# Where the second norm's transposes, its scale and two chunks of dequantisation stand in the order of an attention and feed-forward kernel

## What is computed

```python
x = x + attention(layernorm(x))     # first norm, "n1"
x = x + ffn(layernorm(x))           # second norm, "n2"

# attention, per batch and chunk of 128 tokens, 4 heads of 128
q, k, v = x @ Wq + bq, x @ Wk + bk, x @ Wv + bv
k = k / max(norm(k), 1e-12)
beta, alpha = softplus(x @ Wbeta + bbeta), sigmoid(x @ Walpha + balpha)
cla = cumsum(log(alpha + 1e-6))                  # within the chunk
attn = (q @ k.T) * beta.T * where(causal, exp(cla - cla.T), 0)
y_local = attn @ v
y = y_local + (q @ state.T) * exp(cla)
state = state * exp(cla_end) + v.T @ (k * beta * exp(cla_end - cla))

# feed-forward, 4-bit weights with a scale for 32 numbers, 4096 hidden
gate, up = x @ Wg.T, x @ Wu.T
out = (gelu_tanh(gate) * up) @ Wd.T
```

## Time and profile before

| | us |
|---|---|
| median of 3 runs | 1176.11 (1175.02 to 1176.43) |
| the profiled execution | 1177.4 |
| its span, first to last instruction | 1175.6 |
| TensorE busy with matmuls | 1152.5 (98%) |
| VectorE busy | 838.0 (71%) |
| GpSimd (POOL) busy | 503.1 (43%) |
| ScalarE busy | 394.8 (34%) |

### The profile page before, as it was taken

One profiled execution on the slowest core, in us unless ns is written; L12 is line 12 of the kernel. 1 busy time (PEld: TensorE's weight loads), 2 busy tenths in 40 slices (PEclk: granted clock), 3 DMA queues, 4 the chain that ended last, 5 costly groups with the idle time before them and its releaser, 6 DMA issues.

```text
span 1175.6 us, 19512 instructions
## 1 busy us (share of the span) xinstructions
PE 1152.5 (98%) x7756; PEld 757.4 (64%) x7756; DVE 838.0 (71%) x1387; ACT 394.8 (34%) x831; POOL 503.1 (43%) x503
## 2 busy tenths in 40 slices
PE   6999999999989999999999999999999999999998
PEld 3565554656534444777777777777777777777775
DVE  7778554544865664887788778877887787777554
ACT  3343432433332232333333333333333333332221
POOL 3267232322445773425542563366335634462110
PEclk9999999999999999999999999999999999999999
DMA  8012000000010001110011001100110011000111
GB/s 295 2 47 82 22 24 28 19 14 5 20 54 18 19 18 37 33 41 19 19 37 37 19 19 37 37 19 19 37 37 19 19 37 37 19 23 23 37 37 63
DMA packets 22635, 41.94 MB, mean 36 GB/s; under 512 B 2640, under 2 KB 2704, under 8 KB 22544
## 3 DMA queue, kind: packets, MB, share of 16 engines
q1 hardware_dynamic: 22544, 40.70, 10.7%
HBM read 36.46 MB, written 4.23 MB: 35 GB/s over the span
## 4 chain that ended last, share of the span: by engine, by line
PE 90%; DVE 5%; POOL 2%; issue 1%; ACT 1%; DMA 1%; SPq 0%; DVEq 0%; POOLq 0%
PE ps L445 37%; PE ps L472 27%; PE ps L408 14%; PE ps L313 7%; PE ps L282 1%; DVE bigA L774 1%; PE ps L367 1%; POOL WR L1188 1%; DMA WR<-wqkv 1%; PE ps L361 1%; POOL kn_s L1156 1%; PE ps L350 1%; PE ps L374 0%; DVE wf L963 0%; DVE X L887 0%
## 5 line engine op out<-in xcount | busy, mean ns | idle before, releaser
L472 PE MATMUL ps<-WR,ihl_s 128*128 128x512 f16 x816 | 185.9, 379 | 0.0
L408 PE MATMUL ps<-XT,WR 128*128 128x512 f16 x768 | 172.0, 382 | 3.0 <-DVE X L928 3.0
L472 PE MATMUL ps<-WR,vv 128*128 128x512 f16 x720 | 164.7, 379 | 0.0
L445 PE MATMUL ps<-XT,WR 128*128 128x256 f16 x1152 | 157.1, 273 | 0.0
L445 PE MATMUL ps<-REG,WR 128*128 128x256 f16 x1152 | 157.1, 273 | 0.0
L928 DVE SCALAR_TENSOR_TENSOR X<-ps,X 128x512 f32<-128x512 f32 x128 | 88.0, 689 | 79.0 <-PE ps L472 76.9
L408 PEld LDWEIGHTS ps<-XT,WR 128*128 128x128 f16 x768 | 75.4, 98 | 94.7 <-DVE X L928 3.5
L472 PEld LDWEIGHTS ps<-WR,ihl_s 128*128 128x128 f16 x816 | 79.9, 98 | 85.3
L445 PEld LDWEIGHTS ps<-XT,WR 128*128 128x128 f16 x1152 | 112.7, 98 | 33.5
L1172 POOL TENSOR_TENSOR ihl_s<-fw,ihl_s 128x512 f16<-128x512 f32 x51 | 63.5, 1264 | 136.1 <-ACT ihl_s L606 136.1
L445 PEld LDWEIGHTS ps<-REG,WR 128*128 128x128 f16 x1152 | 112.7, 98 | 13.0
(11 more groups left out here) (166 smaller groups left out, 1874.1 us busy)
## 6 DMA issues: line engine op xcount, KB each, us to landing
load<-codes SPq DMA_DIRECT2D x48, 256.0 KB
load<-scales SPq DMA_DIRECT2D x48, 256.0 KB
y<-X SPq DMA_DIRECT2D x16, 256.0 KB, 2.0
bigA<-cla SPq DMA_DIRECT2D x14, 256.0 KB, 3.2
WR<-wqkv SPq DMA_DIRECT2D x3, 1024.0 KB, 10.9
X<-x SPq DMA_DIRECT2D x3, 1024.0 KB, 13.1
X<-x SPq DMA_DIRECT2D x4, 256.0 KB, 3.4
bigC<-bv SPq DMA_DIRECT2D x1, 256.0 KB, 5.8
```

The source lines that it names most:

```text
L408: mm = eng.matmul(bank[:, :], buf[:, wp, o + kt, 128 * j:128 * j + 128], XT[:, xp, kt, 512 * b:512 * b + 512], start=(n == 0), stop=(n == 11))
L445: mm = eng.matmul(half_bank(kind, name), w(wp, kt), x(xp, kt), start=(n == 0), stop=(n == 5))
L472: mm = eng.matmul(PS[bank][:, :], ih[:, ip, 128 * tt:128 * tt + 128], buf[:, wp, 8 + j, :], start=(m == 0), stop=(m == 11))
```

## The change

TensorE: in the steps T = 5 to 7 and 9 to 11 the transposes follow all projections and the tile; at T = 8 and 12 they follow the projections and three of the four down products, at T = 4 they stay behind the first two projections. Behind the loop they stand between the second and the third down product. ScalarE and VectorE take their halves in the matching order. POOL makes the norm's scale as the first thing in `head`. The dequantisation of chunks 6 and 7 moves from behind the loop into the steps T = 13 and 14, with the bit instructions of chunks 6, 7 and 8 at the ends of the steps T = 12, 13 and 14.

```diff
+DEQUANTED = (0, 1, 2, 3, 5, 7, 13, 14)
@@ TensorE
                 head(T)
                 if T == 0:
                     decay(1)
-                for f in fill[:2]:
-                    qkv(*f)
-                if not fill:
+                if i >= 0 and i % 4 == 0:
+                    for f in fill[:2]:
+                        qkv(*f)
+                    if i == 0:
+                        turn("n2", T - 1)
+                    for f in fill[2:]:
+                        qkv(*f)
+                    if i > 0:
+                        for tt in range(3):
+                            down(i // 4 - 1, tt)
+                        turn("n2", T - 1)
+                        down(i // 4 - 1, 3)
                     upgate(i)
-                if T >= 1:
-                    turn("n2", T - 1)
-                for f in fill[2:]:
-                    qkv(*f)
-                if i > 0 and i % 4 == 0:
-                    for tt in range(4):
-                        down(i // 4 - 1, tt)
-                if i >= 0 and fill:
-                    upgate(i)
+                else:
+                    for f in fill:
+                        qkv(*f)
+                    if i > 0:
+                        upgate(i)
+                    if T >= 1:
+                        turn("n2", T - 1)
                 mid(T)
-            for tt in range(3):
+            for tt in range(2):
                 down(2, tt)
             turn("n2", NT - 1)
-            down(2, 3)
+            for tt in range(2, 4):
+                down(2, tt)
@@ ScalarE
-                if T >= 1:
-                    turn("n2", T - 1)
                 for f in fill:
                     project(*f)
+                if T >= 4 and T % 4 == 0:
+                    turn("n2", T - 1)
                 if T >= 4:
                     act_tile(T - 4)
-                if T in (0, 1, 2, 3, 5, 7):
+                if T % 4:
+                    turn("n2", T - 1)
+                if T in DEQUANTED:
                     dequant(dk)
                     dk += 1
-            dequant(6)
             turn("n2", NT - 1)
-            dequant(7)
@@ VectorE
                 weigh(T)
-                for f in fill[:2]:
-                    project(*f)
-                if T >= 1:
-                    turn_low("n2", T - 1)
-                for f in fill[2:]:
-                    project(*f)
-                if i > 0 and i % 4 == 0:
-                    for tt in range(4):
-                        gather(i // 4 - 1, tt)
-                if i >= 0:
+                if i >= 0 and i % 4 == 0:
+                    for f in fill[:2]:
+                        project(*f)
+                    if i == 0:
+                        turn_low("n2", T - 1)
+                    for f in fill[2:]:
+                        project(*f)
+                    if i > 0:
+                        for tt in range(3):
+                            gather(i // 4 - 1, tt)
+                        turn_low("n2", T - 1)
+                        gather(i // 4 - 1, 3)
                     act_tile(i)
-                if T in (0, 1, 2, 3, 5, 7):
+                else:
+                    for f in fill:
+                        project(*f)
+                    if i > 0:
+                        act_tile(i)
+                    if T >= 1:
+                        turn_low("n2", T - 1)
+                if T in DEQUANTED:
                     dq_finish(dk)
                     dk += 1
                 mid(T)
-                if T in (0, 1, 2, 4, 6):
+                if T in (0, 1, 2, 4, 6, 12, 13, 14):
                     dq_bits(dk)
-            dq_bits(6)
-            dq_finish(6)
             apply("n2", NT - 1)
-            dq_bits(7)
+            for tt in range(2):
+                gather(2, tt)
             turn_low("n2", NT - 1)
-            for tt in range(3):
+            for tt in range(2, 4):
                 gather(2, tt)
-            dq_finish(7)
-            gather(2, 3)
             for i in range(12, 32):
-                if i == 12:
-                    dq_bits(8)
                 act_tile(i)
@@ GpSimd, in head(T)
+                if T >= 1:
+                    norm_scale("n2", T - 1)
                 pl.wait_ge(s_ss, T + 1)
...
-                if T >= 1:
-                    norm_scale("n2", T - 1)
                 pl.wait_ge(s_mask, T + 1)
@@ SyncE
-                if T in (0, 1, 2, 3, 5, 7):
+                if T in DEQUANTED:
                     load_chunk(k)
                     k += 1
-            for k in range(8, 48):
+            for k in range(10, 48):
                 load_chunk(k)
```

## The result

| | before, us | after, us |
|---|---|---|
| median of 7 runs each | 1176.24 | 1179.34 |
| the profiled execution, its span | 1177.4, 1175.6 | 1178.5, 1176.8 |

The changed kernel is slower: the ratio is 1.0027, with a 95% interval from 1.0015 to 1.0039. That is 3.1 us more, where 3.8 less were forecast, and it lies outside the range.

A forecast was written before the change was run, and what follows sets the result against it. TensorE, busy 98% of the span, was taken as the bound, so only its waits could be gained. 5.2 - 0.15 - 1.3 = 3.75 us gained gave 1172.4 us, range 1168.5 to 1175.8.

The forecast's parts named there:

- Part 1: Loop, T = 5 to 12: transposes moved later no longer wait for VectorE's normalised rows; 5.2 us gained.
- the second PSUM use and the low half: VectorE's low half ends some 2.9 us after the tile, its PSUM bank is retaken at 4.5: hidden, 1.6 us spare.
- Part 2: POOL's scale ahead of k's scaling: 5.1 us from statistics to attention weighting's end; first four steps gain 0.15 us.
- the stretch: Lengthening of POOL's six small instructions beside VectorE's four bit instructions: 0.7 us taken, bounds 0 and 1.0.
- Part 3: Dequantisation in T = 12 to 14: removes tile 12's 2.99 us wait, brings some 6 us new; loses 1.3 us.
- rival (b): POOL's stretch above 1.0, about 1.2, or a late last transpose: 1.2 us gained, 1174.9 us, no change; chance 0.18.
- (c): POOL begins only when VectorE's bit instructions end, stretch 2.05, deciding from 1.6: slower, 1180.8 us; chance 0.07.

The follow-up runs named there:

- transposes_only: The kernel before with only the loop's order on TensorE, ScalarE and VectorE from the change; POOL and dequantisation as before: 1169.79 us, 0.9944.
- bits_before_stats: The changed kernel with VectorE's four bit instructions ahead of the same step's statistics, not behind them: 1186.94 us in a single execution.
- filler_short: The changed kernel with 11 useless unit-matrix products ahead of y_local's products in each of T = 3 and 15: 1175.93 us, 0.9999.
- dequant_only: The kernel before with only the dequantisation moved into T = 12 to 14 and the changed order behind the loop: 1180.16 us, 1.0032.
- early_dequant: norm_late with chunk 6 multiplied in T = 12, chunk 7 in T = 13, and their bits behind T = 8 and 12: 1169.36 us, 0.9940.
- quiet_dequant: norm_late with chunk 6's multiplication and chunk 7's bits ahead of T = 12's down sums, chunk 7's multiplication in T = 13: 1166.70 us, 0.9920.
- norm_late: The changed kernel with POOL's scale back behind k's scaling; transposes and dequantisation stay moved: 1171.41 us, 0.9957.
- norm_first_only: The kernel before with POOL's scale ahead of k's scaling and nothing else: 1175.54 us, 0.9993.

## Why the prediction was wrong

- **Part 1 was right.** 5.2 us forecast, 5.43 measured in B, and 5.43 again in transposes_only. The waits of the earlier trace rows were all there was to it; the second PSUM use and the low half hid as worked out.
- **Part 2 failed in its size: the stretch, "I take 0.7", with 1.0 as its bound.** It was 1.3, so the path from the statistics was 5.8 us, not 5.1 (0.6 of it by the stretch, 0.1 in the other pieces). I had read it from the earlier trace rows, where POOL's scaling of k began before or in the middle of the bits. Moved, POOL's chain begins 0.1 us behind the statistics, just after the bits begin, and its first three small instructions all fall beside them. The one cause came back six times: in T = 1 (where I had promised 0.75 us gained, and L869 came 0.1 us later instead, as POOL's six took 3.92 us and not the 3.25 of before), 2, 3, 13, 14 and 15. As an estimate that is 0.85 + 0.7 + 0.7 = 2.2 us in A and 3 x 0.7 = 2.1 in C. bits_before_stats shows 1.06 of the stretch to be the bits; 0.23 remain without them. The trace of before had a case that I did not read: behind the loop the scale follows the statistics at once and runs beside chunk 6's bits (0.54 and 0.74 us, where T = 12 has 0.19 and 0.56), which makes 0.53 us of stretch for these two instructions alone.

```profile
316.11 0.54 POOL L1115 TENSOR_SCALAR rs<-mv 128x1 f32<-128x1 f32 x1 [7.20 <-DVE mv L765]
316.73 0.74 POOL L1118 TENSOR_TENSOR rs<-rs,half 128x1 f32<-128x1 f32 x1
```

- **The sum had no term for the clock.** Behind the waits that I had forecast in T = 3 and T = 15 TensorE ran slow, 1.7 and 1.4 us, as filler_short shows. The same column would have shown 0.71 behind the wait of the earlier trace rows, 1.7 us that the change gives back, in an execution that has this drop. Net 1.4 us lost between the two profiled executions.
- These make up the difference: 2.2 + 2.1 + 1.4 = 5.7, and 0.2 gained more in B, against 5.6 between -3.75 and +1.87.
- **Part 3's mechanism held**, VectorE as the bound in T = 13 to 15 and new waits in place of the old one; I had it as a loss of 1.3 us, and 3.1 were measured in C. Alone, with the transposes and the scale as before, it costs 3 to 4 us (dequant_only).
- **The parts aren't a sum.** By the ratios the scale's order alone is worth -0.8 us (no difference), the transposes alone -6.6, the dequantisation alone +3.8; their sum would be -3.6. But with the transposes and the dequantisation moved, the scale has nothing left to gain in B, and costs 8 us.
- **The stretch fell into rival (b), the time into (c).** 1.3 is above the forecast's bound of 1.0 and below the 1.6 from which (c) decides; at (b)'s 0.5 us for each 0.1 it would have left 0.75 us gained, no change. POOL was not shut out as (c) had it: L1130 ends at 91.24 and L1133 at 92.05, both before the bits are over at 92.63. That the kernel came out slower, as only (c) had it, is due to what the sum lacked besides the stretch: the missed gain in T = 1, 0.1 us more in each step, and the clock. So (c)'s sign came true by other means than its own.
- L1171, which takes 0.23 us without the bits, shows 0.66 us beside L953 and ends at 92.80, just behind L953 at 92.71. By the page SBUF — State Buffer of the Trainium skill, section "SBUF: two separate sides", a GpSimd instruction and a VectorE instruction with two inputs in SBUF can hold each other up: the one that starts first has the shared port pair for the whole instruction, and the other waits. This row agrees. What POOL's rows show is a wait for one VectorE instruction at a time, and not for the whole chain, to which I had given 0.07.

## What to carry to other kernels

When an instruction chain is moved, look at what the other engines run at the new place, and not only at its durations at the old one: here short GpSimd instructions took up to three times as long beside VectorE's integer work (0.66 us and 0.23). When the sum puts a new wait of 2 to 3 us on a TensorE that was busy, allow 1.4 to 1.7 us for the clock behind it as something that may or may not come, and look for such a drop behind the waits that the change removes. Put VectorE's extra work where it waits for TensorE by design (here the four down products), and not between a tile and the statistics that the next step needs; the chunk's share on POOL has to stand there too, as early_dequant and quiet_dequant show together.

## What was not expected of the hardware

- Useless products can pay: eleven in each of two waits made the kernel 3.4 us faster (1179.34 to 1175.93), as the granted clock stayed at 1.00 in the windows around both.
- Drops followed waits of 2.66 and of 2.99 us, two waits of 1.3 us with the transposes between them, and in norm_late a single one of 1.78. None followed the 2.69 us before tile 12 in norm_first_only, the 2.30 us at T = 13 in early_dequant, or the two of 1.3 in filler_short. What decides between such cases stays open; no run was made for it.
- By the mean granted clocks, the same program has the drop in one execution and not in another. Of the 50 executions of the kernel before that stand beside the experiments, 15 have a mean granted clock of 1.000 and took 1174.4 to 1175.2 us; the other 35 have 0.997 to 0.999 and took 1175.8 to 1178.2, with nothing in between. The profiled one (1177.4 us) is of the second kind, so the 1.7 us behind tile 12's wait are probably what most executions pay, and not all (where the others lose their time no trace shows). A comparison of two traces can be off by as much.
